# The next slot's first gate and up products in front of the last down product

## The reference, cut to what matters

```python
x = x + 0.5 * _L0_ffn_ref(_layernorm(x), ...)   # router, 16 experts of width 64, a shared one of width 128
x = x + _L0_attn_ref(_layernorm(x), ...)        # linear attention: silu(q), silu(k), no softmax
x = x + 0.5 * _L0_ffn_ref(_layernorm(x), ...)   # the same experts again
x = x + 0.5 * _L1_ffn_ref(_layernorm(x), ...)   # relu MLP of width 512
x = x + _L1_attn_ref(_layernorm(x), ...)        # softmax attention
x = x + 0.5 * _L1_ffn_ref(_layernorm(x), ...)
```

```python
g = jax.nn.silu(jnp.einsum('th,ehi->eti', x, We_gate)); u = jnp.einsum('th,ehi->eti', x, We_up)
ye = jnp.einsum('eti,eih->eth', g * u, We_down);        y = jnp.einsum('te,eth->th', comb, ye)
shared = jax.nn.silu(hidden_states @ Ws_gate) * (hidden_states @ Ws_up) @ Ws_down
return y + shared
```

## Time and profile before

| | |
|---|---|
| median of 3 runs | 1994.09 us (1993.52 to 1995.16) |
| the profiled execution | 1994.67 us, its span 1992.6 us |
| PE busy | 1886.7 us, 95% of the span |
| DVE, ACT, POOL busy | 1540.8, 1176.8 and 670.6 us |
| front half, 62 to 1155 us | PE 1061.14 us busy of 1093.00, granted clock 1.00 |
| back half, 1161 to 1985 us | PE 792.39 us busy of 824.00, granted clock 0.97 |
| one pair of slots (ATT, MLP) | 66.3 us: the 16 residuals xw <- Y,xw start from 106.2 to 1100.5 us |

### The profile page before, as it was taken

One profiled execution on the slowest core, in us unless ns is written; L12 is line 12 of the kernel. 1 busy time (PEld: TensorE's weight loads), 2 busy tenths in 40 slices (PEclk: granted clock), 3 DMA queues, 4 the chain that ended last, 5 costly groups with the idle time before them and its releaser, 6 DMA issues. The chain is left out here.

```text
span 1992.6 us, 34534 instructions
## 1 busy us (share of the span) xinstructions
PE 1886.7 (95%) x12468; PEld 1312.5 (66%) x12468; DVE 1540.8 (77%) x3888; ACT 1176.8 (59%) x2210; POOL 670.6 (34%) x766
## 2 busy tenths in 40 slices
PE   2999999999999999999999989999999999999997
PEld 1888888888888888888888844444444444444443
DVE  5766866686668666866676669999999999999991
ACT  2344444444444444444444428888888888888884
POOL 2333433343334333433343223333333333333311
PEclk9999999999999999999999969999999999999998
DMA  3000000000000000000010022222232222222210
GB/s 131 7 12 1 12 11 12 1 12 12 11 1 11 12 12 1 11 12 12 1 38 6 7 85 86 86 88 90 91 92 86 86 90 93 90 87 86 86 44 11
DMA packets 49992, 85.81 MB, mean 43 GB/s; under 512 B 6752, under 2 KB 11104, under 8 KB 49760
## 3 DMA queue, kind: packets, MB, share of 16 engines
q1 hardware_dynamic: 47920, 81.85, 13.2%
q10 hardware_dynamic: 1904, 1.78, 0.3%
HBM read 49.26 MB, written 34.87 MB: 42 GB/s over the span
## 5 line engine op out<-in xcount | busy, mean ns | idle before, releaser
L1490 DVE TENSOR_REDUCE b_nm<-b_MX 128x1 f32<-128x512 f32 x1024 | 652.0, 684 | 44.6 <-PE b_MX L1598 24.5
L1383 ACT ACTIVATE b_pr<-b_ST 128x512 f32<-128x512 f32 x1024 | 552.4, 611 | 92.0 <-PE b_ST L1586 89.9
L514 ACT ACTIVATE s<-G 128x512 f32<-128x512 f32 x306 | 182.5, 596 | 350.7 <-PE G L834 348.0
L839 PE MATMUL Y<-w_wd,h 128*128 128x128 f32 x2448 | 329.2, 277 | 17.4 <-DVE h L677 16.1
L668 DVE TENSOR_TENSOR su<-U,s 128x512 f32<-128x512 f32 x272 | 187.1, 688 | 191.4 <-PE U L834 112.8
L839 PEld LDWEIGHTS Y<-w_wd,h 128*128 128x128 f32 x2448 | 305.8, 192 | 33.2 <-DVE h L677 23.9
L1598 PE MATMUL b_MX<-b_kt,b_qt 32*128 32x512 f32 x768 | 236.5, 504 | 2.4 <-DVE b_nm L1490 2.4
L1586 PE MATMUL b_ST<-b_qt,b_kt 32*128 32x512 f32 x768 | 214.7, 494 | 2.8 <-ACT b_pr L1383 1.5
L1586 PEld LDWEIGHTS b_ST<-b_qt,b_kt 32*128 32x128 f32 x768 | 83.1, 181 | 195.0 <-ACT b_pr L1383 141.1
L677 DVE TENSOR_TENSOR h<-C,su 128x512 f32<-128x512 f32 x272 | 188.1, 692 | 9.3
L832 PE MATMUL G<-xh,w_wgh 128*128 128x512 f32 x306 | 145.2, 475 | 0.0
(11 more groups left out here) (295 smaller groups left out, 3705.6 us busy)
## 6 DMA issues: line engine op xcount, KB each, us to landing
b_kt<-staging SPq DMA_DIRECT2D x48, 256.0 KB, 3.1
b_qt<-staging SPq DMA_DIRECT2D x48, 256.0 KB, 3.5
staging<-e_khi SPq DMA_DIRECT2D x32, 256.0 KB, 2.9
staging<-e_qhi SPq DMA_DIRECT2D x32, 256.0 KB, 2.9
xin<-in_x SPq DMA_DIRECT2D x17, 256.0 KB, 2.8
mid<-xo SPq DMA_DIRECT2D x16, 256.0 KB, 2.0
staging<-e_klo SPq DMA_DIRECT2D x16, 256.0 KB, 2.9
staging<-e_qlo SPq DMA_DIRECT2D x16, 256.0 KB, 2.9
```

The costliest lines, as they stand in the source:

```text
L514: nc.scalar.activation(sbuf_s[n % 2][:], G[n % 2][:], ACT.Silu).then_inc(act_done.sem, 1)
L839: mm = pe.matmul(bank[:, t], hid[:, t], wd, start=(first and t == 0), stop=True, skip_group_check=True)
L1383: nc.scalar.activation(pr[k % 2][:, j], bank[:].rearrange("p a b -> p (a b)"), ACT.Exp, scale=SM_SCALE).then_inc(used["st"].sem, 1)
L1490: nc.vector.tensor_reduce(nm[g % 2][:, c:c + 1], bank[:].rearrange("p a b -> p (a b)"), AX.X, ALU.max).then_inc(used["mx"].sem, 1)
```

## The change

On PE the gate and up products of n = 0 of the next slot leave that slot's start and stand in front of the last down product of the slot before. In an MLP slot the last `mlp_down` moves from behind the up product of n = 8 to between gate and up. In an ATT slot `side_transposes` moves behind the down product of the same step. On DVE `activated` of n = 0 moves in front of the main residual of the slot before, and `side_parts` stands directly in front of `total`. On ACT `scores` is done ahead of the side work of its step, which in an MLP slot puts it ahead of the last hidden activation. Three waits are added: the silu of n = 0 for `up_used`, the gate product of n = 0 for `act_done`, and `activated` of n = 0 for `down_done`.

```diff
@@ ACT, slot @@
                     if n >= 2:
                         act.wait_ge(up_used.sem, up_used.at(i, g0 + n - 1))
+                    elif n == 0 and up_used.at(i, g0) > 0:
+                        act.wait_ge(up_used.sem, up_used.at(i, g0))
                     nc.scalar.activation(sbuf_s[n % 2][:], G[n % 2][:], ACT.Silu).then_inc(act_done.sem, 1)
...
+                    if prepare and n == steps["logits"] + 1:
+                        scores(m + 1, i)
                     if side == ATT:
...
-                        if n == steps["logits"] + 1:
-                            scores(m + 1, i)
@@ DVE, activated @@
+                if n == 0 and down_done.at(i, g0 - 2) > 0:
+                    dve.wait_ge(down_done.sem, down_done.at(i, g0 - 2))
                 out = h[0] if n == 0 else su[n % 2]
@@ DVE, slot @@
-                if side:
-                    side_parts(m, i)
...
-                    activated(m, n, i)
+                    if n > 0:
+                        activated(m, n, i)
                     if n == 0:
                         if side:
+                            side_parts(m, i)
                             total(stats_s, mv_s, smv_ready)
...
                 if prepare:
+                    activated(m + 1, 0, i)
                     main_residual(m, i)
@@ PE @@
+            def gate(m, n, i):
+                g0 = NT * m
+                if n >= 2:
+                    pe.wait_ge(act_done.sem, act_done.at(i, g0 + n - 1))
+                elif n == 0:
+                    pe.wait_ge(xl_ready.sem, xl_ready.at(i, m + 1))
+                    if m >= 0:
+                        pe.wait_ge(act_done.sem, act_done.at(i, g0))
+                product(G[n % 2], w["wgh"][:, n], w["wgl"][:, n], xh[m % 2], xl[m % 2]).then_inc(gate_ready.sem, 1)
+
+            def up(m, n, i):
+                if up_used.at(i, NT * m + n) > 0:
+                    pe.wait_ge(up_used.sem, up_used.at(i, NT * m + n))
+                product(U, w["wuh"][:, n], w["wul"][:, n], xh[m % 2], xl[m % 2]).then_inc(up_ready.sem, 1)
...
                 for n in range(NT):
...
                     if n >= 1:
+                        gate(m, n, i)
+                        if side == MLP and n == NT - 1:
+                            mlp_down(m, FT - 1, i)
+                        up(m, n, i)
...
-                    if n == 2 and side:
+                    if n == 2 and side == MLP:
                         side_transposes(i, m)
...
-                        if 5 <= n < 5 + FT:
+                        if 5 <= n < 4 + FT:
                             mlp_down(m, n - 5, i)
...
                     if side == ATT:
+                        if n == 2:
+                            side_transposes(i, m)
...
+                if prepare:
+                    gate(m + 1, 0, i)
+                    up(m + 1, 0, i)
                 moe_down(m, NT - 1, i)
```

More of the change, by code:

```diff
@@ L801, in _ @@
                 f(-1, 0)
+            activated(-1, 0, 0)
             slot(-1, 0, None, None, True)
@@ L948, in first_batch @@
                     mm.then_inc(first_v.sem, 1)
+            def gate(m, n, i):
[11 more added lines that the diff above has]
+                product(U, w["wuh"][:, n], w["wul"][:, n], xh[m % 2], xl[m % 2]).then_inc(up_ready.sem, 1)
             def slot(m, i, side, prepare):
                 g0, a, steps = NT * m, nth(m), PREPARE[side or MLP]
-                high, low = xh[m % 2], xl[m % 2]
-                pe.wait_ge(xl_ready.sem, xl_ready.at(i, m + 1))
                 for n in range(NT):
-                    if n >= 2:
-                        pe.wait_ge(act_done.sem, act_done.at(i, g0 + n - 1))
-                    product(G[n % 2], w["wgh"][:, n], w["wgl"][:, n], high, low).then_inc(gate_ready.sem, 1)
                     if n >= 1:
-                        pe.wait_ge(up_used.sem, up_used.at(i, g0 + n))
-                    product(U, w["wuh"][:, n], w["wul"][:, n], high, low).then_inc(up_ready.sem, 1)
+                        gate(m, n, i)
+                        if side == MLP and n == NT - 1:
+                            mlp_down(m, FT - 1, i)
+                        up(m, n, i)
                     if n == 0:
@@ L1002, in _ @@
             logits(-1, 0)
+            gate(-1, 0, 0)
+            up(-1, 0, 0)
             slot(-1, 0, None, True)
```

## The result

The changed kernel takes 1981.96 us (median of 4 runs, 1981.63 to 1983.05), the kernel before 1993.8 us (4 runs, 1993.52 to 1995.16). The ratio is 0.9943 with a 95% interval of 0.9928 to 0.9957. It is faster by about 12 us, or 0.6%; forecast were 1982.2 us, in a range of 1973 to 1990.

What follows compares the result with a forecast made beforehand. The chain behind the main residual was taken to limit what PE gains. 16 x 0.77 at MLP ends, plus 1.2 at the last, minus 16 x 0.1 at ATT ends: 11.9 us gained, 1982.2 us, range 1973 to 1990.

Steps and rivals of the forecast that it cites:

- PE's pieces: PE at slot ends: prices of single products, summed to 5.22 us from last gate row to comb's transposes, before 6.44.
- T: PE's transposes of comb at a slot's start; forecast 1.22 us earlier at MLP ends, 0.69 at ATT ends.
- The chain as the bound: Behind the MLP end: kvu waits for the chain from the main residual to xls, so gains 0.88 us, not 1.22.
- Rival 1: Both boundaries: no chain binds, all that the comb transposes gain stays, 31.8 us, so 1962.3; chance 0.05.
- Act0 out of the chain: DVE: n = 0 multiplication of h leaves the space between stats_s and mv_s; residual to mv_s 1.63 us, before 2.12.
- the rival that ended slower: Residual to mv_s: the 0.49 us counted back does not return, so 1998.5 us; chance 0.06.
- The ATT end: ATT to MLP boundary: the 0.69 us gained is spent waiting at z's transposes; 0.1 lost, 16 times.
- rival 3: All links at their slow end, residual 0.73 behind act0, more restarts: gain 2.8, 1991.3 us, no measurable change; chance 0.10.
- The cover: MLP end: the moved mlp_down alone covers the last up product's wait for su; early scores costed at nothing.
- The collision: ATT end: DVE's operation on comb waits out POOL's og on the shared SBUF port; it keeps its 0.93 us.
- rival 2: ATT end: the DVE-POOL collision goes away, comb is ready 0.71 sooner, 11.4 us more gained, 1970.8; chance 0.07.
- the last boundary: MLP end into the last slot: no side work behind it, so it keeps about 1.2 us.

Runs made afterwards that it cites:

- e5: Changed kernel with the ATT slots' side_transposes back ahead of the second down product: 1988.07 us.
- e10: Changed kernel with the third down product of ATT slots ahead of the first kvu product: 1976.2 us.
- e1: Changed kernel with gate, up and activated of n = 0 hoisted only where an MLP slot ends, not at ATT ends: 1978.99 us.
- e7: Changed kernel with main statistics of MLP slots and the slot ahead of all one step earlier, n = 1: 1973.16 us.
- e11: Changed kernel plus early main statistics, later MLP side_transposes and the early third down product in ATT slots, hoist only at MLP ends: 1972.0 us.
- e4: Changed kernel with only the last mlp_down put back behind the last up product; scores stays early: 1980.2 us.
- e3: Changed kernel with the last mlp_down and scores both put back; the hoist stays at both boundaries: 1994.68 us.
- e6: Changed kernel without the second POOL operation on og (og + ub), so the attention's output lacks its bias term: 1969.86 us.

## Why the prediction was right, point by point

**PE's pieces.** The 5.22 us from the last gate row to T were worked out piece by piece from five rows and came out as 5.22. T, the residual and mv_s at the MLP end were put 5.22, 5.41 and 7.04 behind that row and stand 5.22, 5.43 and 7.07 behind it. At the ATT end the forecast in its own time was T 3.67, residual 4.15 and mv_s 5.78 behind down7; measured are 3.70, 4.16 and 5.79.

**The chain as the bound.** The step on which the size rests, that kvu gains what mv_s gains and not what T gains, held: kvu was put 13.63 behind the gate row and came at 13.67, with the restart of 0.11 as read. Rival 1, in which all that T gains stays, falls with this: kvu keeps 0.84 of 1.22, and behind the ATT end nothing of 0.66 is left. The runs show more than the timeline does: e5 (less work in the wait for zs, 6.6 us lost) and e10 (ready work in the wait for xls, 6.1 us gained) could not both happen unless PE was waiting there.

**Act0 out of the chain.** Residual to mv_s was forecast as 1.63, against 2.12, and is 1.64 and 1.63. That rules out the rival that ended slower, whose condition was that this time would not come back.

**The ATT end.** A loss of up to 0.14, taken as 0.1, was forecast; it is 0.08 in the timeline, and 1.2 us over 16 boundaries in e1. The reason given, z as the last wait, fits the runs: e7, where z is early, gets 7.3 us back, and in e11 the hoist there is worth 10.3 us behind three moves of which that is one. The hoist with z alone early, and without it, was not compared. Act0 to residual, for which rival 3 took 0.73, is 0.60 here (302.15 to 302.75).

**The cover.** The mlp_down alone was called enough, and scores was costed at nothing. The first was not tried alone; e4 shows that scores alone is enough, and e3 that one of them is needed: without either, the hoist with the side_transposes moved makes the stretch 2.4 us longer than before. The text should have said this of scores: in the kernel before s of n = 7 stood behind two table loads and ended at 332.76, which the trace showed.

**The collision.** It stayed where it was (0.96), as forecast, so rival 2 did not come about by the change; e6 made it come about, and it was worth the 11.4 us that the prediction gave it.

**The sum.** Small misses hide each other. In the stretch the gain is 11.3 us against the 11.9 of the sum: the pairs give 16 x 0.60 = 9.6 for 10.7, the last boundary about 1.5 for 1.2. That the median came within 0.3 us of the forecast is in part luck, since medians of the kernel before alone lie between 1992.3 and 1994.4. A pair of slots gained 0.60, against 0.67 forecast (0.77 - 0.1). The timeline gives 0.84 at kvu, 0.11 of it back in the restart and 0.08 at z, 0.65; the other 0.05 is spread over the rest of the pair. The last boundary gave more than 1.2: T gains 1.21 there, and from T to e_xf it is 25.5 us (1123.82 to 1149.3) in place of 25.8 (1134.99 to 1160.8). Of this 0.2 is a wait of the second up product for act0, which the hoist removes and which the last boundary's term left out; the other 0.1 I did not trace. The waits were named rightly but their lengths in the list come out smaller than forecast, 0.37 for comb against 0.5, 0.2 for z against 0.4, and no line at all for xls against 0.4, since the list counts idle time from the end of the last matmul. A matmul of 512 columns ends 0.16 behind the point where the next could have started (0.39 long at a pace of 0.23), and a down product as much (1.05 against 0.89). From start to start comb costs 0.54 (300.86 to 302.29, less 0.89), z 0.37 and xls 0.29.

## What to carry to other kernels

The list of waits names what PE stands for now, not what it will stand for next. Follow the chain behind the step that is moved (here the residual and the side input made of it) from start to start, and price the move by how far the chain's last link shifts. Work on what comes last first: the same hoist was worth -1.2 us over 16 boundaries in front of late steps and +10.3 once three moves had made them early or covered them. Price a wait from start to start; the idle time of a list can be too small (comb, z), missing (xls), or that of the weight loads. Where a chain can't be made shorter, put ready work of the right length in front of the instruction that waits for it.

## What was not expected of the hardware

The two ends of the program varied far more than its middle. In two profiled runs of one kernel the setup ahead of the first residual differs by 1.4 us (72.9 and 74.3) and what follows e_xf by 1.5 us the other way (831.3 and 829.8), while the stretch between them, more than a thousand us, agrees within 0.1 us (1076.4 and 1076.3). Why the ends vary was not looked into.
